# The score as three fp16 products in a two-layer network on one core

## The reference

```python
# layer 0, batch b with expert i = idx[b]
h  = gelu(x @ fc1_w.T + fc1_b)                  # 512 x 2048
x  = x + concat(h @ fc2_w.T + fc2_b,            # 384 features
                h @ experts_w[i].T + experts_b[i])  # 128 features
# layer 1
s  = tanh(x @ W1 + b1) @ v                      # one score a token
p  = softmax over tokens l of s[l], masked by the batch's type:
     l <= j, l >= j, or l != j
x  = x + (p @ x) / count(mask)
```

## Time and profile before

| | |
|---|---|
| median of 3 runs | 1356.64 us (1356.3 to 1356.75) |
| profiled execution | 1356.64 us, of which the span of instructions 1354.8 us |
| mean granted clock of TensorE | 1.000 |
| busy, of the span | TensorE 99%, VectorE 91%, ScalarE 64% |
| busy DMA engines, by slice | 8 and 4 tenths in the first two of 40, 0 to 2 tenths after |

### The profile page before, as it was taken

One profiled execution on the slowest core, in us unless ns is written; L12 is line 12 of the kernel. 1 busy time (PEld: TensorE's weight loads), 2 busy tenths in 40 slices (PEclk: granted clock), 3 DMA queues, 4 the chain that ended last, 5 costly groups with the idle time before them and its releaser, 6 DMA issues.

```text
span 1354.8 us, 22001 instructions
## 1 busy us (share of the span) xinstructions
PE 1347.6 (99%) x8734; PEld 874.3 (65%) x8734; DVE 1230.8 (91%) x2057; ACT 866.6 (64%) x1493; POOL 0.2 (0%) x4
## 2 busy tenths in 40 slices
PE   9999999999999999999999999999999999999998
PEld 5458476584856758476584756748567584765856
DVE  7988889899898999989899898998989899898998
ACT  4868748376593856848377583756838468483753
POOL 0000000000000000000000000000000000000000
PEclk9999999999999999999999999999999999999999
DMA  8410020110201102011110201102021020200001
GB/s 294 150 48 22 0 71 24 48 48 1 78 17 63 32 8 79 9 62 32 45 50 1 79 17 55 41 0 78 17 63 32 13 77 6 71 24 15 25 10 55
DMA packets 29192, 62.98 MB, mean 46 GB/s; under 512 B 5922, under 2 KB 6690, under 8 KB 26658
## 3 DMA queue, kind: packets, MB, share of 16 engines
q1 hardware_dynamic: 28658, 61.05, 13.7%
q10 hardware_dynamic: 432, 0.53, 0.1%
HBM read 44.79 MB, written 16.78 MB: 45 GB/s over the span
## 4 chain that ended last, share of the span: by engine, by line
PE 96%; DVE 4%; ACT 0%; issue 0%; DVEq 0%
PE ps L398 15%; PE ps L399 15%; PE ps L400 15%; PE ps L317 14%; PE ps L319 14%; PE ps L318 14%; PE ps L430 1%; PE ps L288 1%; PE ps L435 1%; PE ps L598 1%; PE ps L299 1%; PE ps L303 1%; PE ps L301 1%; PE ps L426 1%; PE ps L425 1%; PE ps L424 1%
## 5 line engine op out<-in xcount | busy, mean ns | idle before, releaser
L400 PE MATMUL ps<-hl,w2h 128*128 128x512 f16 x768 | 291.0, 379 | 0.0
L399 PE MATMUL ps<-hh,w2h 128*128 128x512 f16 x768 | 291.0, 379 | 0.0
L398 PE MATMUL ps<-hh,w2l 128*128 128x512 f16 x768 | 291.0, 379 | 0.0
L317 PE MATMUL ps<-xh,w1h 128*128 128x256 f16 x960 | 261.7, 273 | 0.0
L318 PE MATMUL ps<-xl,w1h 128*128 128x256 f16 x960 | 261.7, 273 | 0.0
L319 PE MATMUL ps<-xh,w1l 128*128 128x256 f16 x960 | 261.7, 273 | 0.0
L650 ACT ACTIVATE g<-ps,b1s,ds 128x512 f32<-128x512 f32 x240 | 173.4, 773 | 99.0 <-PE ps L319 99.0
L317 PE MATMUL ps<-xh,ch 128*128 128x256 f16 x720 | 196.4, 273 | 0.0
L319 PE MATMUL ps<-xh,cl 128*128 128x256 f16 x720 | 196.3, 273 | 0.0
L318 PE MATMUL ps<-xl,ch 128*128 128x256 f16 x720 | 196.2, 273 | 0.0
L1064 DVE SCALAR_TENSOR_TENSOR hl<-g,ix,hh 128x512 f16<-128x512 f32 x244 | 179.2, 747 | 1.6
(11 more groups left out here) (208 smaller groups left out, 2348.4 us busy)
## 6 DMA issues: line engine op xcount, KB each, us to landing
xr<-in_xT SPq DMA_DIRECT2D x62, 256.0 KB, 3.1
er<-in_ew SPq DMA_DIRECT2D x15, 1024.0 KB, 6.3
out<-xr SPq DMA_DIRECT2D x60, 256.0 KB, 2.4
raw<-in_w SPq DMA_DIRECT2D x28, 256.0 KB, 6.1
er<-in_w SPq DMA_DIRECT2D x3, 1024.0 KB, 10.1
xr<-in_ew SPq DMA_DIRECT2D x1, 1024.0 KB, 6.2
out<-er SPq DMA_DIRECT2D x3, 256.0 KB, 2.5
xr<-in_xT ACTq DMA_DIRECT2D x2, 256.0 KB, 5.1
```

The costliest lines, as they stand in the source:

```text
L317: mm(to, wh, mh, start=i in (1, 5) and c == 0, stop=False, skip_group_check=True)
L398: mm(po(b, o), wl, hh[:, k, :], start=False, stop=False, skip_group_check=True)
L399: mm(po(b, o), wh, hh[:, k, :], start=False, stop=False, skip_group_check=True)
L400: m = mm(po(b, o), wh, hl[:, k, :], start=False, stop=k == NH - 1, skip_group_check=True)
```

## The change

The score of batches 0 to 14 is formed from fp16 parts. v comes as one column (`vcol`), is scaled by a power of two of its own (column `vc` = 17 of `mx`, `ex`, `ix`) and split into `vh` and `vl`, both [128, 128] with equal columns, which lie in the place of `avs`. `att` is multiplied by 2^13 (`grow`) and split into `hh[:, 0, :]` (ScalarE, behind tanh) and `hl[:, 0, :]` (VectorE, `attention_low`), which batch b no longer needs at that time. The score is three fp16 products into `pa`, and `keep_score` multiplies by `vinv`, the inverse of both scales. `avs` itself is loaded only for the last batch, behind the last use of `vh` and `vl`. On VectorE the 13 pooling steps of the opening are dealt out otherwise around the additions: 1 + 4 + 3, two additions, 2, one addition, 3 become 1 + 4 + 4, one addition, 2, one addition, `attention_low`, one addition, 2. A few small tiles (`ones`, `abs_`, `rz`, `grow`, `vcol`, `vinv`) become columns of one.

```diff
--- before.py
+++ after.py
@@ -66,7 +66,11 @@
     x2h = [nc.alloc_sbuf_tensor_at(f"x2h{c}", [P, S], f32r, offset=at) for c, at in enumerate(x2h_at)]
     fifth = sb("fifth", [P, 2, HALF])
     aws_at = here()
-    aws, avs = sb("aws", [P, KD, A]), sb("avs", [A, P])
+    aws, avs_at = sb("aws", [P, KD, A]), here()
+    avs = sb("avs", [A, P])
+    vh, vl = (nc.alloc_sbuf_tensor_at(n, [A, P], f16, offset=avs_at + at) for n, at in (("vh", 0), ("vl", 2 * P)))
+    cols = sb("cols", [P, 16])
+    ones, abs_, vcol, vinv, grow, rz = (cols[:, lo:hi] for lo, hi in ((0, 1), (1, 2), (2, 3), (3, 4), (4, 5), (8, 12)))
     early_at = here()
     early = sb("early", [P, A])
     awl = [sb("awl0", [P, A], f32r), sb("awl1", [P, A], f32r),
@@ -91,9 +95,8 @@
     zFi, zFx = zF[:, 1:S + 1], zF[:, 0:S]
     zBx = zB[:, 1:S + 1]
     io = sb("io", [P, S], f16)
-    b1s, b2s, ebs, abs_ = sb("b1s", [P, NH]), sb("b2s", [P, 3]), sb("ebs", [P, 2]), sb("abs", [P, 1])
+    b1s, b2s, ebs = sb("b1s", [P, NH]), sb("b2s", [P, 3]), sb("ebs", [P, 2])
     lcol, scol, shift, limit = sb("lcol", [P, 4]), sb("scol", [P, 4]), sb("shift", [P, 4]), sb("limit", [P, B])
-    rz, ones = sb("rz", [P, 4]), sb("ones", [P, 1])
     idxs, pts = sb("idxs", [1, B], i32), sb("pts", [P, B], i32)
     ptf, e0, e1, e2 = (early[:, 64 + i * B:64 + (i + 1) * B] for i in range(4))
     cF, cS, cB, cntp, cntq, cD = (sb(n, [P, B]) for n in ("cF", "cS", "cB", "cntp", "cntq", "cD"))
@@ -101,9 +104,9 @@
 
 
     oneb = sb("oneb", [P, P], bf16)
-    NC = 17
+    NC = 18
     mx, ex, ix, lift = sb("mx", [P, NC], bf16), sb("ex", [P, NC]), sb("ix", [P, NC]), sb("lift", [P, NC])
-    w1c, w2c = 3, 11
+    w1c, w2c, vc = 3, 11, 17
 
     def hc(b):
         return 14 * (b % 2)
@@ -190,6 +193,8 @@
                                        sems("ein", 2), sems("ebin", 2))
     (e0_in, idx_in, pt_in, b1_in, b2_in, aw_in, ab_in, av_in, io_in, eye_in, lcol_in) = (
         sem(n) for n in ("e0in", "idxin", "ptin", "b1in", "b2in", "awin", "abin", "avin", "ioin", "eyein", "lcolin"))
+    vcol_in, vmax_done, vh_done, vl_done, vinv_done, atth_done, attl_done = (
+        sem(n) for n in ("vcolin", "vmax", "vh", "vl", "vinv", "atth", "attl"))
 
     (bits_set, summed, tile_done, p1, p5, p6, p7, p3, fc2_done, half_done, attended, score_done, nat_done, cols_done,
      totals_done, piece_done) = (sem(n) for n in (
@@ -430,9 +435,12 @@
                 mm(pa, aws[:, c, :], chunk(b, c), start=start, stop=stop).then_inc(attended)
 
         def score(b):
-            e.wait_ge(tanh_done, b + 1)
-            e.wait_ge(av_in, 16)
-            mm(pa, avs[:, :], att, start=True, stop=True).then_inc(score_done)
+            e.wait_ge(atth_done, b + 1)
+            e.wait_ge(vl_done, 1)
+            mm(pa, vl[:, :], hh[:, 0, :], start=True, stop=False)
+            mm(pa, vh[:, :], hh[:, 0, :], start=False, stop=False)
+            e.wait_ge(attl_done, b + 1)
+            mm(pa, vh[:, :], hl[:, 0, :], start=False, stop=True).then_inc(score_done)
 
         def opening(b):
 
@@ -477,6 +485,7 @@
 
         def score_half(v, n):
             e.wait_ge(tanh_done, LAST + 1 + v)
+            e.wait_ge(av_in, 16)
             mm(pf[n][:, 0:HALF], avs[:, :], att[:, HALVES[v]], start=True, stop=True).then_inc(score_done)
 
 
@@ -526,7 +535,8 @@
         attend(0, 0)
         fc2(0, 2, range(0, 8))
         e.wait_ge(bound_step, 6)
-        chain_sum(9, hc(1), hc(1) + 3)
+        e.wait_ge(vmax_done, 1)
+        chain_sum(9, hc(1), vc + 1)
         fc2(0, 2, range(8, 16))
         attend(0, 1)
         fc2(0, 3, range(0, 12))
@@ -770,6 +780,8 @@
             else:
                 e.wait_ge(sums_low_done, 2)
             act(att, pa, ACT.Tanh, bias=abs_[:, 0:1]).then_inc(tanh_done)
+            e.wait_ge(tanh_done, b + 1)
+            copy(hh[:, 0, :], att, grow[:, 0:1]).then_inc(atth_done)
 
         def keep_score(b):
             e.wait_ge(score_done, b + 1)
@@ -777,7 +789,8 @@
                 e.wait_ge(pool_step, pool_value(b - 1, 11))
             else:
                 e.wait_ge(sums_low_done, 1)
-            copy(sc, pa).then_inc(scored)
+            e.wait_ge(vinv_done, 1)
+            copy(sc, pa, vinv[:, 0:1]).then_inc(scored)
 
         def exponentials(b, lo):
             e.wait_ge(pool_step, pool_value(b, 12))
@@ -875,6 +888,8 @@
         split_expert_high(0, 1)
         sums_high(0)
         sums_high(1)
+        e.wait_ge(ix_done, 9)
+        copy(vh[:, :], vcol.broadcast_to([A, P]), scale_of(vc)).then_inc(vh_done)
         split_expert_high(0, 2)
         split_x_high(1, X11)
         evacuate(0, 2)
@@ -1018,7 +1033,7 @@
         def chain_scale(n, lo, hi):
 
             e.wait_ge(summed, n)
-            e.wait_ge(ones_set, 7)
+            e.wait_ge(ones_set, 8)
             stt(ex[:, lo:hi], pss[:, lo:hi], TINY, lift[:, lo:hi], ALU.max, ALU.mult).then_inc(pss_read)
             bits = ex[:, lo:hi].bitcast(i32)
             e.wait_ge(pss_read, n)
@@ -1036,7 +1051,7 @@
             ts(is2[:, b % 2, lo:hi], ix[:, col:col + hi - lo], ix[:, hc(b):hc(b) + 1], None, ALU.mult).then_inc(ds2_done)
 
         def batch_scales(b):
-            chain_scale(8 + b, hc(b), hc(b) + 3)
+            chain_scale(8 + b, hc(b), hc(b) + 3 if b > 1 else vc + 1)
             fc1_scale(b, 8 + b, 0, PAIRS)
             out_scales(b, 8 + b, 3, 4, ec(b))
             out_scales(b, 8 + b, 0, 3, w2c)
@@ -1146,6 +1161,10 @@
             low_part(flat(w1l[:, 2 * p + 1, 0:2, :]), one, c, flat(w1h[:, 2 * p + 1, 0:2, :])).then_inc(sums_low_done)
             e.wait_ge(three_high, p + 1)
             low_part(flat(cl[:, p, :, :]), three, c, flat(ch[:, p, :, :])).then_inc(sums_low_done)
+
+        def attention_low(b):
+            e.wait_ge(atth_done, b + 1)
+            low_part(hl[:, 0, :], att, grow[:, 0:1], hh[:, 0, :]).then_inc(attl_done)
 
         def pads():
             e.wait_ge(sums_low_done, 8)
@@ -1288,7 +1307,8 @@
         eng.memset(ones[:, :], 1.0).then_inc(ones_set)
         eng.memset(oneb[:, :], 1.0).then_inc(ones_set)
         eng.memset(x5[:, :, KD:KD + 1], 1.0).then_inc(ones_set)
-        for lo, hi, power in ((0, 2, -14), (2, 11, -12), (11, 16, -14), (16, 17, -12)):
+        eng.memset(grow[:, :], 2.0 ** 13).then_inc(ones_set)
+        for lo, hi, power in ((0, 2, -14), (2, 11, -12), (11, 16, -14), (16, 18, -12)):
             eng.memset(lift[:, lo:hi], 2.0 ** power).then_inc(ones_set)
         w1_biggest(0)
         e.wait_ge(x_in[0], 16)
@@ -1372,6 +1392,8 @@
         for q in range(4):
             w2_low(2, 0, q)
         weight_sums_first(0)
+        e.wait_ge(vcol_in, 16)
+        column(vc, vcol[:, :]).then_inc(vmax_done)
         bounds(1)
         weight_sums_second(0)
         expert_low(0, 0)
@@ -1381,6 +1403,9 @@
         expert_low(0, 1)
         sums_low(0)
         x_low(1, X11)
+        e.wait_ge(vh_done, 1)
+        low_part(vl[:, :], vcol.broadcast_to([A, P]), scale_of(vc), vh[:, :]).then_inc(vl_done)
+        ts(vinv[:, :], ex[:, vc:vc + 1], 2.0 ** -13, None, ALU.mult).then_inc(vinv_done)
         combine(1, T3)
         combine(1, T4)
         expert_low(0, 2)
@@ -1394,6 +1419,7 @@
         add_first(1, 0)
         weight_sums_first(4)
         add_second(1, 0)
+        attention_low(0)
         add_first(1, 1)
         sums_low(3)
         weight_sums_second(4)
@@ -1461,12 +1487,13 @@
             x2_low(b, 2)
             pool(1)
             pool(4)
-            pool(3)
+            pool(4)
             add_first(b + 1, 0)
+            pool(2)
             add_second(b + 1, 0)
+            attention_low(b)
+            add_first(b + 1, 1)
             pool(2)
-            add_first(b + 1, 1)
-            pool(3)
 
 
         def natural_low(c, n):
@@ -1576,7 +1603,7 @@
         dma(b2s[:, :], b2).then_inc(b2_in, 16)
         dma(pts[:, :], pt).then_inc(pt_in, 16)
         dma(abs_[:, :], ab).then_inc(ab_in, 16)
-        dma(avs[:, :], av).then_inc(av_in, 16)
+        dma(vcol[:, :], av[:, 0:1], allow_slow_non_contiguous=True).then_inc(vcol_in, 16)
         dma(io[:, :], iota).then_inc(io_in, 16)
         dma(lcol[:, :], tokens).then_inc(lcol_in, 16)
         dma(aws[:, :, :], aw).then_inc(aw_in, 16)
@@ -1598,6 +1625,8 @@
             else:
                 e.wait_ge(attended, nth_chunk(LAST - 1, 2))
                 dma(aws[:, 0:3, :], aw[:, 0:3, :]).then_inc(aw_in, 16)
+                e.wait_ge(score_done, LAST)
+                dma(avs[:, :], av).then_inc(av_in, 16)
             if b > 1:
                 for c in (1, 2, 3):
                     store(b - 2, c)
```

## The result

The changed kernel took 1353.09 us (median of 9 runs, 1352.77 to 1354.58), the kernel before in the same sessions 1356.71 (9 runs, 1356.18 to 1357.75). The ratio is 0.9975 with a 95% interval of 0.9964 to 0.9985: faster by 3.6 us or 0.27%, where 3.2 us and 0.24% were forecast. The profiled execution took 1352.9 us, its span is 1351.1.

A forecast was written before the change was run, and what follows sets the result against it. TensorE's sum of products was taken to bound the batch loop: 15 scores, each 0.21 us shorter, save 3.2 us, with nothing added elsewhere, so 1356.64 - 3.2 = 1353.4 us; the range was 1352.8 to 1354.8.

The forecast's parts named there:

- The bound: Batch loop: the sum of TensorE's products sets the end; ScalarE or VectorE work costs nothing until a product waits.
- The price: Score on TensorE: fp32 0.86 us, three fp16 products 0.65; saving 0.21 a batch, 3.2 us over 15 scores.
- The chain in front: From tanh through the hh copy and attention_low to the third product: operand ready 512.44, wanted 513.02, spare 0.58 us.
- the slower rival: Third product waits for attention_low 0.97 us beyond forecast: 2.7 us more than before, 1359.3 and beyond; chance 0.03.
- The queues: ScalarE and VectorE around the score: moved scan and steps fit idle times of 1.28 and 2.39 us before the additions.
- ends the stretch about 1.5 us earlier: VectorE in the opening: 13 pooling steps before and after, scans now in idle time; TensorE gains nothing.
- Behind the score: keep_score with column scale takes 0.68 us; product1 of pair 2 does not wait, spare 0.34 to 0.43.
- Start and tail: Start's extra instructions are covered, at most 1 us once without covers, taken as 0; whole saving reaches the end.

The follow-up runs named there:

- again: The changed kernel once more, without an edit, against the kernel before: 1352.95 us, ratio 0.9974.
- more_fillers: The changed kernel with 25 instead of 17 idle products in front of the last batch's pooling products: 1352.89 us, ratio 0.9974 to the kernel before.
- before_again: The kernel before itself, unedited, for a second profile of its start: 1356.59 us, ratio 0.9998.
- layout_alone: The kernel before with only the change's layout of small tiles and its extra memset, score still fp32: 1356.44 us, ratio 0.9997.
- dealing_alone: The kernel before (fp32 score) with only the pooling steps dealt out as in the change: 1356.6 us, ratio 1.0001.

## Why the prediction was right

**The bound.** TensorE's sum sets the loop: shown from three sides. One product less in each score took 3.3 us, the side work without the products took nothing off, and the dealing alone did nothing. In 14 scores the stretch is 1144.9 to 1145.0 us long in three profiles with the change (after, again, more_fillers) and 1147.9 to 1148.2 in four of kernels with the fp32 score that nothing holds (before, before_again, layout_alone, dealing_alone).

**The price.** 0.86 against 3 x 0.217 was read from distances from start to start; the profile after has 0.65, and 2.94 us over 14 scores. Three products with three loads of all 128 rows took 0.65, with the loads of the second and third starting beside the product in front, and the score with one product and one load less took about 0.22 less. That contradicts the rule of the Trainium skill (TensorE: Matmul & The Clock Gate, "What overlaps and what doesn't") that a load runs beside a product in flight only where the two use different row groups, by which the loads would add up and the change would be slower.

**The chain in front.** Forecast and profile, with 1.42 between the two clocks (512.59 became 511.17): copy to hh 0.76 after tanh, found 0.73; low part ready at 512.44, found 512.40; third product unheld, 0.58 to spare, found 0.62. Putting a scan in front used it up to 0.05 beyond, and so confirmed its size; putting two there gave the slower rival, 16.7 us over the change and 13.0 over the kernel before.

**The queues.** Idle time before the two additions 0.2 and 0.7, found 0.29 and 0.69. That VectorE "ends the stretch about 1.5 us earlier" and "TensorE gains nothing from that" held against the kernel before: the first pooling step behind the stretch's 13 started at 515.53 there and at 512.43 + 1.42 = 513.85 here, 1.7 earlier. What the forecast did not say is what the moved steps are for: with the low part in the queue and the old dealing, a wait stands at the second addition behind the low part and costs 14 us. I had looked at the readers of the additions inside the opening, and not at the first one behind it. VectorE's busy time rose by 18.2, not by 11. The low parts are 15 x 0.75 = 11.3, as forecast; what was left out is the dealing, which alone made the same 2057 instructions busy for 7.9 us more. A likely reason, not shown, is that records back to back overlap (a scan's record is 1.22 long and the next instruction starts 1.13 after it), and the steps that moved into idle time overlap less.

**Behind the score.** keep_score with a column scale 0.68, found 0.69; product1 unheld with 0.34 to 0.43, found 0.42; a copy more there cost 0.37 a score.

**Start and tail.** Both at nothing, to within the rest below: the start's instructions are all in idle time (2.32 us are left of the 2.72 in front of the first addition), and the tail follows. The measured 3.6 to 3.7 are 0.4 to 0.5 above 15 x 0.21. In the first two profiles that difference stands where the first loads land and in the last store, but both move by 0.3 to 0.4 in the same program, so one profile of each can't place it. The medians of two sessions agree with each other, and without the longer executions the layout alone stood 0.3 lower, so a part of it may belong to the program; which instruction would do it stays open. The forecast had no term for this rest.

## What to carry to other kernels

Where one engine has no waits at all, a change is worth its price in distances from start to start on that engine, and everything else is a question of spares: list for each new wait when the operand is ready and when its turn comes. Follow an instruction that is put into a full queue past the stretch that you edit, to the first place where the queue was idle before; lateness is handed on to every reader until then. Steps that can be moved into idle time are what pays for it, even if moving them alone shows nothing.

## What the runs showed of the hardware

In 6 of 18 executions the changed kernel stood 1.5 us higher. Two profiles of it caught both cases. In the last batch TensorE does 17 idle products, then has nothing for 1.8 us, then the products of the last pooling. A stretch of those, in the execution of the first comparison (from:to, length, busy us and instructions of PE, PEld, DVE, ACT and POOL, then granted clock, share of the DMA engines, GB/s):

```profile
1336.90:1340.40 3.50, 3.50 (x19) 2.96 (x18) 3.29 (x6) 2.87 (x5) 0.00 (x0) 1.00 0.02 5
```

and in that of the second, where the first pooling product started at 1335.58:

```profile
1337.10:1340.60 3.50, 3.50 (x12) 2.93 (x11) 3.30 (x6) 2.83 (x5) 0.00 (x0) 0.51 0.02 5
```

The granted clock is 1.00 in one and 0.51 in the other, that is the lower of its two levels, 1.2 GHz, for nearly all of the stretch; 12 products started in it instead of 19. What TensorE did before was the same in both: 17 idle products in 3.83 us, then nothing for 1.81 and 1.84 us. 3.5 us at half the clock cost about 1.7 by that sum, near the 1.5 seen.

The change did not bring this. The kernel before does the same, in 3 of 19 to 10 of 21 of its executions in a session, 1.1 us above its others, and its two profiles show the same 36 products in 7.22 us and in 8.80 us, the second with a granted clock of 0.53 over 3.5 us of them:

```profile
1338.91 7.22 PE ps L598 x36
```

```profile
1338.83 8.80 PE ps L598 x36
```

With the pause filled it was not seen in 9 executions, which, as said above, may still be chance.
